# Where the low halves of delta and delta*x are subtracted in a fused Mamba and expert layer: 16 subtractions go from GpSimd to VectorE

## The chip, the cores and the metric

The kernel runs on one core of a Trainium2 chip. The time is that of the device for one execution, in microseconds. The core has TensorE (PE, matmuls into PSUM banks), VectorE (DVE), ScalarE (ACT), GpSimd (POOL), and SyncE (SP), whose queue issues most of the DMAs. The engines run side by side and meet only at semaphores; each takes its own instructions strictly in the order of the program.

## What is computed

For 32 sequences of 256 tokens with 128 channels, `x + mamba(layernorm(x)) + moe(layernorm(x))`. The heavy part is the state scan of the Mamba branch:

```python
delta = softplus(delta + dt_proj_b)
def step(s, inp):
    d_t, u_t, B_t, C_t = inp
    dA = jnp.exp(d_t[..., None] * A)
    s = s * dA + (d_t * u_t)[..., None] * B_t[:, :, None, :]
    y_t = jnp.einsum('bhdn,bhn->bhd', s, C_t)
    return (s, y_t)
```

There are 256 inner channels of 16 states each, so 4096 recurrences per sequence. The expert branch sends each token to one of 8 experts of up to 1024 tokens (two layers, 512 hidden) and weighs the result by the gate.

## The kernel before, in words

The tokens are cut in 16 chunks of 512. The main part is one body per chunk, 0 to 15, written once per kind and run in two hardware loops: body 0 alone, bodies 1 to 8 (each with one expert's matmuls besides), bodies 9 to 14 and body 15 (with the gathering of expert rows instead). I call 1 to 8 expert bodies and 9 to 15 gather bodies.

A body has 32 slots, `w` = 0 to 31, 16 for each half of the inner channels. A slot handles 128 recurrences over 512 tokens:

1. PE spreads delta*x over the 128 rows (`spread_du`, L1182) and delta (`spread_delta`, L1189), two slots ahead. Both read `dsp`, where each value stands as a high and a low part on different partitions, so that one fp32r matmul adds the two.
2. ACT takes the exponential (L762).
3. DVE multiplies delta*x by B (`spread_u`, L902, written one slot ahead) and then runs the scan (L972).
4. POOL multiplies the scanned state by C (L578). In body 0 and body 15 DVE does a share of these.
5. Every fourth slot PE sums four such products (`sum_quad`, L1204).

PE's matmuls for the next chunk's projections (L1114, L1117, L1127), for its delta (L1135 to L1138) and for the experts (L1160, L1164, L1171) stand between the slots by the hand-written tables `STAGE_A` and `FFN`. They go through two PSUM banks in turn, and a tile waits until the tile two before it was read (`claim`).

The values that `dsp` holds are made once per half chunk: ACT writes delta to `dd[:, 0]` (L720), POOL multiplies it by x into `dd[:, 1]` (L534) and clears the first step of each sequence (L538), ACT rounds both to `hi` (L726), and `lo = dd - hi` is one subtraction over 128x1024 elements. That last one is `split_low`. Then the SP queue copies both parts to `dsp` (`stack`, L434, four DMAs). The table

```python
SOFTPLUS = {"act": (2, 3, 4, 5), "scale": (9,), "zero": (10,), "low": (13,), "high": (13,)}
```

counts slots from the delta projection, so `split_low` stands at slot 7 of a body (for the second half of its own chunk, used from slot 16) and at slot 24 (for the first half of the next chunk, used from its slot 0). Who makes it was decided per body by `low_by_pool`: POOL in the expert bodies, DVE elsewhere. The very first half chunk, ahead of body 0, is POOL's.

Of the kernel before, what the change touches and what calls it, by code (L numbers as in the profile page):

```python
# [86 lines left out]
def bass_mamba_moe(nc, hidden, in_w, conv_w, conv_b, xp_w, dt_w, dt_b, a_log, d_skip, out_w,  # L87
                   wg, w1, b1, w2, b2, consts, out):
    ctx = ExitStack()
    with ctx:  # L90
# [136 lines left out]
        def softplus_slots(hf):  # L227
            v = STAGE_A[f"v{hf}"][0]
            return {what: [v + k for k in after_v] for what, after_v in SOFTPLUS.items()}

        def softplus_now(ch, w, what):

            found = []
            for hf in range(HALVES):
                at = softplus_slots(hf)[what]
                for step, slot in enumerate(at):
                    if slot % SLOTS == w:
                        of = after(ch) if slot < SLOTS else ch
                        if of[0] < CHUNKS:
                            found.append((of, hf, step))  # L240
            return found
# [21 lines left out]
        def per_chunk(ch, n, k):  # L263
            return lin(ch, lambda c: n * c + k)
# [21 lines left out]
        def wait(eng, name, value):  # L286
            if not isinstance(value, int) or value > 0:
                eng.wait_ge(S[name] if isinstance(name, str) else name, value)
# [19 lines left out]
        def delta_in(ch, hf):  # L308

            return ch if hf else before_or_start(ch)  # L310
# [4 lines left out]
        def has_ffn(ch):  # L315
            return FIRST_FFN <= ch[0] < FIRST_FFN + EXP
# [1 line left out]
        def has_combine(ch):  # L318
            return ch[0] >= FIRST_COMBINE

        def low_by_pool(ch):

            return has_ffn(ch)

        def after(ch):
            return (ch[0] + 1, ch[1])

# [3 lines left out]
        def xs_of(ch, hf):  # L331
            return xs[:, ch[0] % 2, hf, :]
# [4 lines left out]
        def head_of(w):  # L337

            return w % QUADS // 2
# [23 lines left out]
        def centre(eng, b):  # L363

            t = slice(b * BT, (b + 1) * BT)
            return eng.tensor_tensor(xn[:, t, :], acc[:, t, :], mean[:, t].unsqueeze(2).broadcast_to([P, BT, DM]),
                                     ALU.subtract)
# [137 lines left out]
        @block.gpsimd  # L505
        def _(pool):
            pool.memset(zero, 0.0).then_inc(S["zero_ready"], 1)
            pool.memset(xin, 0.0).then_inc(S["xin_zeroed"], 1)
            pool.memset(xnT[:, :, 0:TAPS - 1], 0.0).then_inc(S["xin_zeroed"], 1)
            pool.memset(weff[:, :, :], 0.0).then_inc(S["xin_zeroed"], 1)  # L510
            pool.memset(wg_sb[:, EXP:32], 0.0).then_inc(S["xin_zeroed"], 1)
            pool.memset(neg_m, -SP_M)
            pool.memset(neg_t, -SP_T)
            pool.memset(log_t1, LN_C1 - SP_M)
            pool.memset(log_t2, LN_C2 - 2 * SP_M)
            pool.memset(none, 0.0).then_inc(S["xin_zeroed"], 1)
            for b in (1, 3):
                pool.wait_ge(S["sp_chain"], 2 * b + 2)
                pool.wait_ge(S[f"x_loaded{b}"], 16)
                centre(pool, b).then_inc(S["centred_pool"], 1)  # L520
            for b in range(LN_BLK - 1):
                t = slice(b * BT, (b + 1) * BT)
                pool.wait_ge(S["rstd_ready"], b + 1)
                pool.tensor_tensor(xn[:, t, :], xn[:, t, :],
                                   rstd[:, t].unsqueeze(2).broadcast_to([P, BT, DM]),
                                   ALU.mult).then_inc(S["xn_ready"], 1)

            def scale_x(ch, hf):

                wait(pool, "stacked", per_chunk(ch, 128, 64 * hf))  # L530
                if ch == (0, None) and hf == 0:
                    pool.wait_ge(S["ein_zeroed"], 16 * EXP)
                pool.wait_ge(*tile_read(delta_in(ch, hf), f"D{hf}"))
                pool.tensor_tensor(dd[:, 1, :], dd[:, 0, :], xs_of(ch, hf), ALU.mult).then_inc(S["dx_ready"], 1)  # L534

            def zero_first():

                pool.memset(dd[:, 0, :].rearrange("p (s t) -> p s t", s=SEQS)[:, :, 0:1], 0.0  # L538
                            ).then_inc(S["dd_ready"], 1)

            def split_low(ch, hf):

                pool.wait_ge(S["hi_ready"], per_chunk(ch, 2, hf + 1))
                pool.tensor_tensor(lo, dd, hi.bitcast(F32), ALU.subtract).then_inc(S["lo_ready"], 1)

            scale_x((0, None), 0)
            pool.wait_ge(S["dx_ready"], 1)
            zero_first()
            split_low((0, None), 0)

            def gathers(tiles=range(GROUP)):

                for n in tiles:
                    pool.indirect_dma_start(back[:, n, :], None, eout[:, :],  # L554
                                            bass.IndirectOffsetOnAxis(ap=take_now[:, n:n + 1], axis=0),
                                            ).then_inc(S["back_loaded"], 16)

            def body(ch):
                for w in range(SLOTS):
                    hf, hh = w // UNITS, head_of(w)  # L560
                    if w == 1 and has_combine(ch):
                        pool.wait_ge(S["eo_free"], 16 + 32 * EXP)
                        pool.wait_ge(S["take_ready"], lin(ch, lambda c: c - FIRST_COMBINE + 1))

                    span = QUADS if ch[0] == 0 else 1
                    due = lambda what: [x for v in range(w - span + 1, w + 1) if w % span == span - 1
                                        for x in softplus_now(ch, v, what)]
                    zero_now = due("zero")
                    for of, hf_, _ in zero_now:
                        pool.wait_ge(S["dx_ready"], per_chunk(of, 2, hf_ + 1))  # L570
                    if not by_dve(ch, w):
                        if not any(by_dve(ch, v) is False for v in range(w // UNITS * UNITS, w)):
                            pool.wait_ge(*bc_loaded(ch, hf, "c"))
                        if w % UNITS == UNITS - 1 and ch[0] + 1 < CHUNKS:
                            pool.wait_ge(*tile_read(ch, f"bc{w // UNITS}"))
                        pool.wait_ge(S["scan_done"], per_chunk(ch, SLOTS, w + 1))
                        s_now = s_sb[:, w % S_RING, :]
                        pool.tensor_tensor(s_now, s_now, c_of[:, hf, hh, :], ALU.mult).then_inc(S["p_ready"], 1)  # L578
                    if zero_now:
                        zero_first()  # L580
                    if ch[0] == 0:
                        if w == 0:
                            pool.wait_ge(S["routed"], 2)
                        for i in range(w * TILES // SLOTS, (w + 1) * TILES // SLOTS):
                            pool.indirect_dma_start(ein[:, :],  # L585
                                                    bass.IndirectOffsetOnAxis(ap=put_at[:, i:i + 1], axis=0),
                                                    xn[:, i, :], None).then_inc(S["scattered"], 16)
                    for of, hf_, _ in softplus_now(ch, w, "scale"):
                        scale_x(of, hf_)
                    if low_by_pool(ch):  # L590
                        for of, hf_, _ in due("low"):
                            split_low(of, hf_)
                    if GATHER <= w < GATHER + GROUP and has_combine(ch):
                        gathers((w - GATHER,))
                    if ch[0] == CHUNKS - 1 and LAST_GATHER <= w < LAST_GATHER + GROUP:
                        if w == LAST_GATHER:
                            pool.wait_ge(S["take_ready"], TILES // GROUP)
                        gathers((w - LAST_GATHER,))

            chunks(pool, body, lambda: None)  # L600


# [187 lines left out]
        def _(dve):  # L790
# [114 lines left out]
            def split_low(ch, hf):  # L905

                dve.wait_ge(S["hi_ready"], per_chunk(ch, 2, hf + 1))
                dve.tensor_tensor(lo, dd, hi.bitcast(F32), ALU.subtract).then_inc(S["lo_ready"], 1)
# [52 lines left out]
            def body(ch):  # L961
                plan = tiles_of(ch[0])
                for w in range(SLOTS):
# [18 lines left out]
                    for step in range(2):  # L982
                        if w == GATE[step] and ch[0] > 0:
                            gate_half(before(ch), 1, step)
                        if w == UNITS + GATE[step]:
                            gate_half(ch, 0, step)
                    if not low_by_pool(ch):
                        for of, hf_, _ in softplus_now(ch, w, "low"):
                            split_low(of, hf_)
                    if has_ffn(ch) and w == b1_slot:  # L990
                        k = lin(ch, lambda c: (c - FIRST_FFN) * FT)
                        dve.tensor_copy(b1_now[:, :], b1c[:, bass.ds(k, FT)]).then_inc(S["b1_ready"], 1)
# [315 lines left out]
```

## Time and profile before

| | |
|---|---|
| median of 3 runs | 1237.58 us (1233.49 to 1238.75) |
| profiled execution | 1234.84 us, span 1232.9 us |
| busy: PE, DVE, ACT, POOL | 83%, 87%, 60%, 70% of the span |

The span runs from the first to the last instruction that the profiler saw; 1.94 us of the execution lie around it. Busy shares are means over bodies of different kinds, so they don't tell which engine is waited for in a given slot.

### The profile page before, as it was taken

The page shows a single profiled execution, that of the slowest core. Times are in us where ns is not written, and L with a number is a line of the kernel's source. Part 1 is how long each engine was busy: PE and PEld are TensorE (multiplying, and loading weights), DVE is VectorE, ACT ScalarE, POOL GpSimd, SP SyncE. Part 2 cuts the span into 40 slices and gives each one's busy share as a digit, 9 for nine tenths or more (in the row PEclk, how much of TensorE's full clock was granted, in tenths as well). Part 3 has the DMA queues.
Part 4 walks back from the last instruction along what each step waited for, and adds up shares of the span by engine and source line. Part 5 has one row for each costly group of instructions (what it writes and reads, how often), then busy time and mean ns, then how long its engine had stood idle before and what let it go on. Part 6 is the DMA issues. An engine that isn't in the chain of part 4 may idle for free.

```text
span 1232.9 us, 15308 instructions
## 1 busy us (share of the span) xinstructions
PE 1022.4 (83%) x3821; PEld 476.4 (39%) x3821; DVE 1070.5 (87%) x1331; ACT 734.7 (60%) x1117; POOL 858.9 (70%) x708
## 2 busy tenths in 40 slices
PE   0755858999999899999999997888888888888785
PEld 0522324444545454444445453333333333243322
DVE  7647968889898979899898989999898989999996
ACT  2564535767586776767685766556564756555421
POOL 2335788767676867677676769687777868686755
PEclk9988868999999999999999999788887979797765
DMA  6542325243432424342534423442434333343311
GB/s 160 157 94 68 91 79 130 57 99 69 107 80 64 103 62 111 77 94 51 119 68 98 89 57 80 86 86 48 87 71 90 81 73 68 82 85 80 72 36 34
DMA packets 81065, 103.01 MB, mean 84 GB/s; under 512 B 13280, under 2 KB 51072, under 8 KB 81024
## 3 DMA queue, kind: packets, MB, share of 16 engines
q1 hardware_dynamic: 76928, 94.18, 35.3%
q0 software_dynamic: 4096, 8.40, 2.3%
q8 instruction: 12, 0.20, 0.1%
q14 instruction: 29, 0.24, 0.1%
HBM read 18.66 MB, written 16.78 MB: 29 GB/s over the span
## 4 chain that ended last, share of the span: by engine, by line
PE 40%; DVE 24%; issue 22%; POOL 7%; ACT 3%; DVEq 1%; DMA 1%; SPq 1%; POOLq 0%; ACTq 0%
DVE u_sb L902 10%; DVE s_sb L972 8%; PE bank L1204 6%; PE bank L1171 5%; PE bank L1189 5%; PE bank L1127 4%; PE bank L1182 4%; PE bank L1114 3%; POOL expert_in L585 3%; PE bank L1135 2%; PE bank L1136 2%; PE bank L1137 2%; POOL s_sb L578 2%; PE bank L1147 2%; DVE g_sb L860 2%
## 5 line engine op out<-in xcount | busy, mean ns | idle before, releaser
L578 POOL TENSOR_TENSOR s_sb<-s_sb,c_of 128x512 f32<-128x512 f32 x480 | 628.5, 1315 | 273.2 <-DVE s_sb L972 265.1
L972 DVE TENSOR_TENSOR_SCAN s_sb<-bank,u_sb 128x512 f32<-128x512 f32 x512 | 620.4, 1212 | 0.0
L762 ACT ACTIVATE bank<-bank,a_neg 128x510 f32<-128x510 f32 x512 | 334.0, 659 | 255.9 <-PE bank L1189 246.4
L902 DVE TENSOR_TENSOR u_sb<-bank,b_of 128x512 f32<-128x512 f32 x512 | 346.2, 676 | 98.7 <-PE bank L1182 94.9
L1182 PE MATMUL bank<-dsp,sel_d 128*128 128x512 f32 x512 | 316.1, 617 | 39.8 <-DVE u_sb L902 20.4
L1189 PE MATMUL bank<-dsp,sel_d 128*128 128x512 f32 x512 | 244.5, 478 | 79.0 <-DVE s_sb L972 71.5
L1182 PEld LDWEIGHTS bank<-dsp,sel_d 128*128 128x128 f32 x512 | 104.6, 204 | 243.4 <-DVE u_sb L902 147.6
L1189 PEld LDWEIGHTS bank<-dsp,sel_d 128*128 128x128 f32 x512 | 106.5, 208 | 195.4 <-DVE s_sb L972 163.0
L1204 PE MATMUL bank<-s_sb,con 128*32 128x512 f32 x1024 | 161.2, 706 | 12.7 <-POOL s_sb L578 6.8
L1114 PE MATMUL bank<-xnT,wx 128*128 (+1 forms) x256 | 128.8, 597 | 0.0
L585 POOL DMA_INDIRECT expert_in<-xn,put_at x64 | 65.6, 1026 | 17.9 <-issue 17.8
L554 POOL DMA_INDIRECT xn<-expert_out,take_now x64 | 66.0, 1031 | 10.5 <-issue 7.4
L726 ACT ACTIVATE hi<-dd 128x1024 fp32r<-128x1024 f32 x32 | 33.9, 1058 | 61.8 <-POOL dd L538 61.8
L1127 PE MATMUL bank<-xs,bcw 128*64 128x512 f32 x64 | 46.7, 822 | 27.5 <-ACT xs L677 27.5
L1171 PE MATMUL bank<-xn 128*128 128x128 f32 x512 | 64.0, 278 | 6.4 <-ACT xn L737 6.4
L1171 PEld LDWEIGHTS bank<-xn 128*128 128x128 f32 x512 | 60.7, 191 | 17.3 <-ACT xn L737 9.9
L534 POOL TENSOR_TENSOR dd<-dd,xs 128x512 f32<-128x512 f32 x32 | 40.9, 1277 | 34.2 <-ACT dd L720 34.1
L1164 PE MATMUL bank<-xn 128*128 128x512 f32 x128 | 64.4, 605 | 0.3
L1114 PEld LDWEIGHTS bank<-xnT,wx 128*128 128x128 f32 x256 | 47.4, 189 | 27.7 <-issue 22.8
L720 ACT ACTIVATE dd<-bank,small 128x512 f32<-128x512 f32 x32 | 22.1, 690 | 52.6 <-PE bank L1138 51.6
L737 ACT ACTIVATE xn<-bank,b_now 128x512 f32<-128x512 f32 x64 | 43.1, 688 | 14.5 <-PE bank L1164 13.9
L1204 PEld LDWEIGHTS bank<-s_sb,con 128*32 128x32 f32 x1024 | 21.4, 114 | 60.0 <-issue 44.9
(140 smaller groups left out, 1045.0 us busy)
## 6 DMA issues: line engine op xcount, KB each, us to landing
b_of<-bc SPq DMA_DIRECT2D x64, 256.0 KB
c_of<-bc SPq DMA_DIRECT2D x64, 256.0 KB
dsp<-hi SPq DMA_DIRECT2D x64, 256.0 KB
dsp<-dd SPq DMA_DIRECT2D x64, 256.0 KB
expert_in<-dd SPq DMA_DIRECT2D x8, 512.0 KB, 6.4
xn<-expert_in SPq DMA_DIRECT2D x8, 512.0 KB, 5.4
xn<-L_ffn_W SPq DMA_DIRECT2D x16, 256.0 KB, 4.6
expert_out<-xn SPq DMA_DIRECT2D x16, 256.0 KB, 2.4
```

The source lines that it names most:

```text
L554: pool.indirect_dma_start(back[:, n, :], None, eout[:, :], bass.IndirectOffsetOnAxis(ap=take_now[:, n:n + 1], axis=0),).then_inc(S["back_l ...
L578: pool.tensor_tensor(s_now, s_now, c_of[:, hf, hh, :], ALU.mult).then_inc(S["p_ready"], 1)
L585: pool.indirect_dma_start(ein[:, :], bass.IndirectOffsetOnAxis(ap=put_at[:, i:i + 1], axis=0), xn[:, i, :], None).then_inc(S["scattered"], 16)
L762: act.activation(d, d, ACT.Exp, scale=a_neg[:, k:k + 1]).then_inc(S["decay_ready"], 1)
L902: dve.tensor_tensor(u_sb[:, w % U_RING, :], du_ps[w % 2][:, :], b_of[:, hf, head_of(w), :], ALU.mult).then_inc(S["u_ready"], 1)
L972: dve.tensor_tensor_scan(s_sb[:, w % S_RING, :], decay_of(w)[:, :], u_sb[:, w % U_RING, :], 0.0, ALU.mult, ALU.add).then_inc(S["scan_done" ...
L1114: mm = pe.matmul(t[:, :], wx[:, hf, part, :], xnT[:, seqs, part:part + SEQ], start=(part == 0), stop=(part == TAPS - 1))
L1127: pe.matmul(t[0:4 * NS, :] if name[0] == "b" else t[:, :], w[:, hf, :], xs_of(ch, hf), start=True, stop=True).then_inc(S["misc_pe"], 1)
L1171: mm = pe.matmul(t[:, part * P:(part + 1) * P], hT[:, f, part * P:(part + 1) * P], w2_sb[:, f, :], start=(f == 0), stop=(f == FT - 1))
L1182: pe.matmul(du_ps[w % 2][:, :], sel_d[:, group_of(w), :, :].rearrange("k n d -> k (n d)"), dsp[:, hf, head_of(w), 1, :], start=True, stop= ...
L1189: pe.matmul(decay_of(w)[:, :], sel_d[:, group_of(w), :, :].rearrange("k n d -> k (n d)"), dsp[:, w // UNITS, head_of(w), 0, :], start=True ...
L1204: mm = pe.matmul(y_ps[q * 32:(q + 1) * 32, :], con[:, K_SUM + 32 * r:K_SUM + 32 * (r + 1)], s_sb[:, (QUADS * k + q) % S_RING, :], start=(r ...
```

## The change

`low_by_pool` and its call in the GpSimd program go; the DVE program calls `split_low` in every body. The 16 subtractions of bodies 1 to 8 (two each) move. The one ahead of body 0 stays with POOL.

```diff
-        def low_by_pool(ch):
-
-            return has_ffn(ch)
...
                     for of, hf_, _ in softplus_now(ch, w, "scale"):
                         scale_x(of, hf_)
-                    if low_by_pool(ch):
-                        for of, hf_, _ in due("low"):
-                            split_low(of, hf_)
                     if GATHER <= w < GATHER + GROUP and has_combine(ch):
...
-                    if not low_by_pool(ch):
-                        for of, hf_, _ in softplus_now(ch, w, "low"):
-                            split_low(of, hf_)
+                    for of, hf_, _ in softplus_now(ch, w, "low"):
+                        split_low(of, hf_)
```

The lines move up a little in the changed file: before's L902, L908 and L972 are L895, L901 and L965 there, POOL's L578 is L574. First DVE's order at slot 7 of an expert body, before: slot 7's scan, then slot 9's product with B, then slot 8's scan.

```order
L972 SCALAR_TENSOR_TENSOR s_sb<-bank1,u_sb 128x512
L901 REGISTER_ALU
L902 TENSOR_TENSOR u_sb<-bank4,b_of 128x512
L288 REGISTER_ALU
L972 SCALAR_TENSOR_TENSOR s_sb<-bank2,u_sb 128x512
```

The same place in the changed program, where `dd<-dd,hi` is `split_low`:

```order
L965 SCALAR_TENSOR_TENSOR s_sb<-bank1,u_sb 128x512
L900 REGISTER_ALU
L901 TENSOR_TENSOR dd<-dd,hi 128x1024
L894 REGISTER_ALU
L895 TENSOR_TENSOR u_sb<-bank4,b_of 128x512
L288 REGISTER_ALU
L965 SCALAR_TENSOR_TENSOR s_sb<-bank2,u_sb 128x512
```

The subtraction now stands between slot 7's scan and slot 9's product, ahead of slot 8's scan. At slot 24 it stands in the same way, ahead of the addition that reads the expert's first output tile (`expert_out`, L880 before, L873 after):

```order
L901 TENSOR_TENSOR dd<-dd,hi 128x1024
L894 REGISTER_ALU
L895 TENSOR_TENSOR u_sb<-bank3,b_of 128x512
L965 SCALAR_TENSOR_TENSOR s_sb<-bank1,u_sb 128x512
L894 REGISTER_ALU
L895 TENSOR_TENSOR u_sb<-bank4,b_of 128x512
L965 SCALAR_TENSOR_TENSOR s_sb<-bank2,u_sb 128x512
L869 REGISTER_ALU
L871 REGISTER_ALU
L872 ISA
L873 TENSOR_TENSOR xn<-bank6,xn 128x512
```

On POOL before, it stood behind the product of slot 7 and ahead of that of slot 8; those products now follow one another.

```order
L578 TENSOR_TENSOR s_sb<-s_sb,c_of 128x512
L544 TENSOR_TENSOR dd<-dd,hi 128x1024
L576 REGISTER_ALU
L578 TENSOR_TENSOR s_sb<-s_sb,c_of 128x512
```

## Rows read from the trace of the kernel before

**Rows 1.** The page: busy us (share of the span) and instructions.

```profile
PE 1022.4 (83%) x3821; PEld 476.4 (39%) x3821; DVE 1070.5 (87%) x1331; ACT 734.7 (60%) x1117; POOL 858.9 (70%) x708
```

**Rows 2.** Groups of instructions by line, whole span: busy us, mean ns | idle before.

```profile
L544 POOL TENSOR_TENSOR dd<-dd,hi 128x1024 fp32r<-128x1024 f32 x17 | 40.1, 2358 | 1.2 <-ACT hi L726 1.2
...
L908 DVE TENSOR_TENSOR dd<-dd,hi 128x1024 fp32r<-128x1024 f32 x15 | 19.0, 1269 | 14.1 <-ACT hi L726 14.1
```

**Rows 3.** Busy by stretch: bodies 1, 2, 5 and 12 (us; PE, PEld, DVE, ACT, POOL).

```profile
184.50:258.40 73.90, 67.67 (x277) 34.73 (x276) 61.14 (x73) 47.74 (x74) 54.56 (x44) 0.94 0.38 88
258.40:328.00 69.60, 64.97 (x275) 33.15 (x274) 60.36 (x73) 47.19 (x73) 48.58 (x38) 0.98 0.38 84
...
464.10:532.20 68.10, 63.45 (x275) 32.52 (x275) 60.10 (x73) 46.97 (x73) 48.57 (x38) 1.00 0.39 85
...
943.70:1011.90 68.20, 58.46 (x187) 24.05 (x186) 63.11 (x82) 41.43 (x63) 52.76 (x44) 0.85 0.38 77
```

**Rows 4.** DVE's timeline, body 5, scans of slots 7 and 8 (start, duration).

```profile
478.03 1.21 DVE L972 TENSOR_TENSOR_SCAN s_sb<-bank,u_sb 128x512 f32<-128x512 f32 x1
...
479.74 1.21 DVE L972 TENSOR_TENSOR_SCAN s_sb<-bank,u_sb 128x512 f32<-128x512 f32 x1
```

**Rows 5.** DVE's timeline, body 12, slots 7 and 8.

```profile
958.17 1.21 DVE L972 TENSOR_TENSOR_SCAN s_sb<-bank,u_sb 128x512 f32<-128x512 f32 x1
959.30 1.24 DVE L908 TENSOR_TENSOR dd<-dd,hi 128x1024 fp32r<-128x1024 f32 x1
...
961.07 1.21 DVE L972 TENSOR_TENSOR_SCAN s_sb<-bank,u_sb 128x512 f32<-128x512 f32 x1
```

**Rows 6.** DVE's groups in 479.3 to 499.9, body 5, slots 8 to 19.

```profile
L902 DVE TENSOR_TENSOR u_sb<-bank,b_of 128x512 f32<-128x512 f32 x12 | 8.0, 668 | 0.0
```

**Rows 7.** DVE's timeline, body 5, its two longest waits, and the read at slot 26.

```profile
502.74 0.69 DVE L902 TENSOR_TENSOR u_sb<-bank,b_of 128x512 f32<-128x512 f32 x1 [2.20 <-PE bank L1182]
...
516.01 0.66 DVE L880 TENSOR_TENSOR xn<-bank,xn 128x512 f32<-128x512 f32 x1
...
521.44 0.69 DVE L902 TENSOR_TENSOR u_sb<-bank,b_of 128x512 f32<-128x512 f32 x1 [2.60 <-PE bank L1182]
```

**Rows 8.** PE's timeline, body 5.

```profile
489.82 0.49 PE L1182 MATMUL bank<-dsp,sel_d 128*128 128x512 f32 x1 [0.78 <-DMA dsp<-dd]
...
495.39 0.50 PE L1189 MATMUL bank<-dsp,sel_d 128*128 128x512 f32 x1
...
518.14 1.98 PE L1164 MATMUL bank<-xn 128*128 128x512 f32 x4
```

**Rows 9.** The SP queue's timeline, body 5, first of each `stack`.

```profile
482.93 0.51 SPq L434 DMA_DIRECT2D dsp<-hi  x1
...
517.22 0.51 SPq L434 DMA_DIRECT2D dsp<-hi  x1
```

**Rows 10.** DVE's timeline, body 1, slot 9.

```profile
206.94 0.69 DVE L902 TENSOR_TENSOR u_sb<-bank,b_of 128x512 f32<-128x512 f32 x1 [1.82 <-PE bank L1182]
```

**Rows 11.** Two stretches of body 2; third number from the end: granted clock.

```profile
271.60:275.00 3.40, 1.84 (x6) 0.56 (x5) 3.40 (x5) 3.22 (x5) 2.72 (x3) 1.00 0.00 0
275.00:278.40 3.40, 3.40 (x7) 1.60 (x8) 2.67 (x5) 2.79 (x4) 3.40 (x3) 0.50 0.07 16
```

**Rows 12.** DVE's timeline, body 2, slots 9 to 11, its waits.

```profile
277.61 0.69 DVE L902 TENSOR_TENSOR u_sb<-bank,b_of 128x512 f32<-128x512 f32 x1 [0.73 <-PE bank L1182]
...
281.89 0.69 DVE L872 TENSOR_TENSOR acc<-bank,acc 128x512 f32 x1 [0.63 <-PE bank L1147]
```

**Rows 13.** The same slots of body 12.

```profile
964.16 0.69 DVE L902 TENSOR_TENSOR u_sb<-bank,b_of 128x512 f32<-128x512 f32 x1 [0.17 <-PE bank L1182]
...
968.20 0.69 DVE L872 TENSOR_TENSOR acc<-bank,acc 128x512 f32 x1 [0.51 <-PE bank L1147]
```

**Rows 14.** POOL's timeline, body 9, the product under way as slot 7 ends.

```profile
751.30 1.29 POOL L578 TENSOR_TENSOR s_sb<-s_sb,c_of 128x512 f32<-128x512 f32 x1
```

**Rows 15.** DVE's timeline, the same moment.

```profile
752.08 1.60 DVE L908 TENSOR_TENSOR dd<-dd,hi 128x1024 fp32r<-128x1024 f32 x1
```

## The prediction

> **What bounds the kernel now.** I read the page first. VectorE is the busiest engine, 87% of the span [rows 1], and the change gives it more. A mean over the span doesn't say who waits, so I went on to the busy times by body. An expert body in the steady state takes 68.1 us, of which DVE is busy 60.10 and POOL, from which the work comes, 48.57 [rows 3]. Bodies 3 to 8 all read 68.0 to 68.2, so one of them can stand for six. Bodies 1 and 2 are longer, with a granted clock of 0.94 and 0.98 where the steady ones have 1.00.
>
> Then DVE's own timeline, to see where its 8 idle us lie. In body 5 the twelve L902 from slot 8 to slot 19 have no idle time before them [rows 6]: there DVE is the chain, one slot every 479.74 - 478.03 = 1.71 us [rows 4], and PE, ACT and POOL wait for it. The idle time comes in two lumps, 2.20 us behind slot 19 and 2.60 us behind slot 27, both ended by PE's `spread_du` [rows 7]. There PE is the chain: between the slots it works off delta and the experts' matmuls. So a body is DVE's in slots 7 to 19 and PE's from about slot 24 on, and the two subtractions fall one into each part.
>
> **What the change removes.** Sixteen L544 on POOL, 2.358 us each, 37.7 us of POOL's time [rows 2]. I cost this at nothing. L544 makes POOL's next products late by up to its own length, and DVE doesn't wait once in the slots behind it [rows 6], so PE's sums of those products never held DVE up. The work that hides it is DVE's own. If the lag did matter, the gain could be up to 2.4 us at each of the 16 places; rows 6 exclude it at slot 7.
>
> **What it adds at slot 7.** One subtraction on DVE ahead of the product and scan of slot 8. The gather bodies show this very sequence. Body 12 goes from scan 7 to scan 8 in 961.07 - 958.17 = 2.90 us [rows 5], where body 5 takes 1.71 [rows 4]. The price is 1.19 us a place. The group's mean of 1.269 [rows 2] is the busy time, which overlaps with its neighbours, and would give little more. All later work of DVE in the body is pushed back. Nobody absorbs it before slot 19, since DVE has no idle time there. Does the wait of 2.20 us behind slot 19 absorb it? I say no. PE comes to that lump from L1189 at 495.39 [rows 8], which waits for slot 16's scan: PE's burst starts when DVE lets it, so it starts 1.19 us later and ends 1.19 us later.
>
> The input `hi` should not be late. The 14.1 us of waiting for ACT before L908 [rows 2] lie in body 0, where POOL is held by the scattering of rows.
>
> **What it adds at slot 24.** The same 1.19 us, ahead of a stretch that is PE's. DVE then waits less: of the 2.60 us before L902 at 521.44 [rows 7] some is used up. Two things could let the delay through. PE's L1164 at 518.14 [rows 8] needs the bank that DVE's L880 reads at 516.01 for 0.66 us [rows 7]; 1.19 us later it ends at 517.86, 0.28 us ahead. And the SP queue stores the expert's tile before it issues `stack`; this starts at 517.22 [rows 9] and would start 1.19 us later, for matmuls that PE reaches at the end of the body. I cost slot 24 at nothing, with 1.19 us a place as the bound if that cover is gone.
>
> **What is earlier.** At slot 7 the four DMAs of `stack` begin when the low part is there, 482.93 now [rows 9] and about 480.4 then. PE waits 0.78 us for them at 489.82 [rows 8]. That wait should go, but DVE doesn't wait for PE there [rows 6], so it buys nothing.
>
> **Bodies 1 and 2.** In body 1 DVE stands idle 1.82 us at slot 9, waiting for PE [rows 10]; 1.19 us fit in, so body 1 costs 0. In body 2 the granted clock was 0.50 for 3.4 us, which is the 1.2 GHz level, after a stretch as long in which PE was busy for 1.84 us only [rows 11]. DVE then waited 0.73 + 0.63 = 1.36 us [rows 12]. The gather bodies have both the fall of the clock and DVE's subtraction at this place, and there DVE waits 0.17 + 0.51 = 0.68 us [rows 13]: a later DVE hides part of a slower PE. So body 2 costs 1.19 + 0.68 - 1.36 = 0.51.
>
> **The clock in bodies 3 to 8.** They run the same program as body 2 and show no fall; body 12 and its like do at the same slots. Which body falls depends on where it stands in time, and the change moves all of them. I take half of the six, 3 x 0.68 = 2.0 us, with bounds of none and six (4.1).
>
> **The port.** At 752.08 L908 took 1.60 us instead of 1.24 [rows 5, 15], and a product had been running on POOL since 751.30 [rows 14]: 0.36 us more. In a steady expert body POOL is up with DVE at slot 7 and its product starts after DVE's subtraction, so I add nothing; the bound is 7 x 0.36 = 2.5 us. The Trainium skill says why in *SBUF — State Buffer*, section "Who interferes with whom": a VectorE instruction with two SBUF inputs and a GpSimd instruction share one pair of ports as an exclusive lock, and the one that starts first holds it to its end. The trace agrees, and by that rule POOL's product would be the one to wait here.
>
> **The sum.** 0 (body 1) + 0.51 (body 2) + 6 x 1.19 = 7.14 (bodies 3 to 8) + 2.04 (clock) = 9.7 us. On the profiled execution's 1234.84 that is 1244.5. The median of the runs shown is 2.7 us above that execution, so 1237.58 + 9.7 = 1247.3 us, which I forecast.
>
> **The rivals.**
>
> *Hidden at slot 7 too.* If PE's burst behind slot 19 starts from something other than DVE, its 2.20 us wait absorbs the delay. Cost 0, or -0.7 if body 2's clock stays up: 1237. For it speaks that both lumps of idle time are longer than 1.19 us; against it, that L1189 at 495.39 waited for DVE. Chance 0.12.
>
> *Faster: the low part was late.* PE waits 0.78 us for `dsp` at slot 16. If this is the chain in each of the eight bodies, 8 x 0.78 = 6.2 us come back and DVE's delay is hidden: 1231.3. It decides if DVE is found waiting for PE's spread of slot 16. In body 5 it isn't. The Trainium skill speaks for this side in *GPSIMD Engine Reference*, section "4.1 Engine selection": two-input elementwise work belongs on VectorE, GpSimd being about half as fast. The rows agree on the ratio, 2358 to 1269 ns [rows 2], but what is gained in engine time is on the engine with room. Chance 0.05.
>
> *Exposed at slot 24 too.* If 0.28 us is too little, or the late `stack` is waited for, 8 x 1.19 = 9.5 us come on top: 1256.8. Chance 0.07.
>
> *The clock falls nearly everywhere.* DVE's late slots leave PE idle in more pieces. If the six steady bodies lose 1.36 us each as body 2 did, without overlap, that is 8.2 in place of 2.0: 1253.4. Body 12's 0.85 [rows 3] shows that the level isn't safe; that PE has 5 us more work in an expert body speaks against. Chance 0.13.
>
> **How the numbers follow.** The forecast's own case has 0.60 and spans +7.7 (no fall of the clock) to +11.7 (six), 1245.3 to 1249.3; 0.03 is left for what I don't see. Three runs of before spread over 5.3 us, so I widen: 1241 leaves out the two low rivals (0.17) and 1254 the one at 1256.8. Half a per cent, 6.2 us, is about what a measurement can tell from no change. Slower takes the rivals above and nearly all of the main case, 0.60 x 0.9 + 0.20 = 0.74; within 0.5% the rest of it and the hidden case, 0.21; faster 0.05.
>
> **What would show it.** In the changed trace: sixteen more of the 128x1024 subtraction on DVE at 1.20 to 1.27 us, only one on POOL; scan 7 to scan 8 of a steady body 2.9 us apart; still no idle time of DVE from slot 8 to 19 except where the clock fell; the 2.20 us wait unchanged and the 2.60 us wait shorter by about 1.2; the 0.78 us wait for the DMA gone; bodies 3 to 8 at 69.2 to 70.0 us; gather bodies as before. The forecast is wrong if the wait behind slot 19 shrinks instead, if the one behind slot 27 doesn't, or if the clock's falls cost more than 4 us.

## The result and the profile after

| | before | after |
|---|---|---|
| median of 9 runs | 1234.63 us (1231.19 to 1238.75) | 1243.37 us (1240.41 to 1245.73) |
| profiled execution | 1234.84 us, span 1232.9 us | 1241.68 us, span 1239.7 us |

The ratio is 1.0066 with an interval of 1.005 to 1.0082: the changed kernel is slower, by 8 to 9 us (the medians differ by 8.7). The forecast was 1247.3 us within 1241 to 1254. Of the 3.9 us by which it lies above the measured median, 3.0 are the median of before itself, which six more runs brought down from 1237.58 to 1234.63; the forecast's +9.7 on the new median would be 1244.3. The two profiled executions differ by 6.8 us.

The page of after answers to [rows 1]: DVE has 16 instructions and 14.8 us more, POOL 16 instructions and 21.7 us less, and the span is longer all the same. The sixteen instructions that left POOL took 37.7 us, yet its busy time fell by 21.7 only: its products (L578 before, L574 after) have become 15.0 us longer in sum. The two lines below are theirs.

```profile
PE 1021.3 (82%) x3821; PEld 479.1 (39%) x3821; DVE 1085.3 (88%) x1347; ACT 734.9 (59%) x1117; POOL 837.2 (68%) x692
```

```profile
L578 POOL TENSOR_TENSOR s_sb<-s_sb,c_of 128x512 f32<-128x512 f32 x480 | 628.5, 1315 | 273.2 <-DVE s_sb L972 265.1 <-POOL dd L534 3.5 <-DMA expert_out<-xn 1.0
...
L574 POOL TENSOR_TENSOR s_sb<-s_sb,c_of 128x512 f32<-128x512 f32 x480 | 643.5, 1344 | 301.5 <-DVE s_sb L965 295.5
```

The groups of the subtraction, answering to [rows 2]: 31 on DVE at a mean of 1253 ns, one left on POOL.

```profile
L901 DVE TENSOR_TENSOR dd<-dd,hi 128x1024 fp32r<-128x1024 f32 x31 | 38.9, 1253 | 14.1 <-ACT hi L719 14.1
...
L540 POOL TENSOR_TENSOR dd<-dd,hi 128x1024 fp32r<-128x1024 f32 x1 | 2.3, 2347 | 1.2 <-ACT hi L719 1.2
```

Then the busy times of after by body, answering to [rows 3]: bodies 1, 2, 3, 4, 5, 7 and 12 (columns as there). The steady expert bodies (4 and 5 here) have gone from 68.0 and 68.1 to 69.0 and 69.1 (69.2 in the rounded window) at a granted clock of 1.00. Bodies 3 and 7 took 69.7 at 0.98. Body 12 takes 68.2 as before.

```profile
184.90:257.40 72.50, 66.51 (x277) 33.80 (x276) 63.52 (x75) 47.70 (x74) 51.83 (x42) 0.96 0.38 89
257.40:326.40 69.00, 64.02 (x275) 32.50 (x274) 62.17 (x75) 47.00 (x73) 45.92 (x36) 1.00 0.39 84
326.40:396.10 69.70, 65.08 (x275) 33.78 (x275) 62.36 (x75) 47.01 (x73) 45.90 (x36) 0.98 0.38 83
396.10:465.10 69.00, 64.01 (x275) 32.50 (x274) 62.18 (x75) 47.01 (x73) 45.91 (x36) 1.00 0.39 84
465.10:534.30 69.20, 64.25 (x275) 32.60 (x275) 62.27 (x76) 47.11 (x73) 45.87 (x36) 1.00 0.38 83
...
603.30:673.00 69.70, 65.09 (x275) 33.69 (x275) 62.35 (x75) 47.11 (x73) 45.93 (x36) 0.98 0.38 83
...
949.70:1017.90 68.20, 57.70 (x188) 24.36 (x187) 63.01 (x82) 41.42 (x63) 52.67 (x44) 0.88 0.37 77
```

DVE's timeline of after in body 5, answering to [rows 4, 7]. The first three lines are slot 7; then the wait behind slot 19, the read of the expert's bank at slot 26, and the wait behind slot 27.

```profile
479.05 1.22 DVE L965 TENSOR_TENSOR_SCAN s_sb<-bank,u_sb 128x512 f32<-128x512 f32 x1
480.18 1.20 DVE L901 TENSOR_TENSOR dd<-dd,hi 128x1024 fp32r<-128x1024 f32 x1
...
481.89 1.22 DVE L965 TENSOR_TENSOR_SCAN s_sb<-bank,u_sb 128x512 f32<-128x512 f32 x1
...
504.80 0.69 DVE L895 TENSOR_TENSOR u_sb<-bank,b_of 128x512 f32<-128x512 f32 x1 [2.18 <-PE bank L1174]
...
519.20 0.68 DVE L873 TENSOR_TENSOR xn<-bank,xn 128x512 f32<-128x512 f32 x1
...
523.48 0.69 DVE L895 TENSOR_TENSOR u_sb<-bank,b_of 128x512 f32<-128x512 f32 x1 [1.88 <-PE bank L1174]
```

Scan 7 to scan 8 is 481.89 - 479.05 = 2.84 us, 1.13 more than before. The wait behind slot 19 is 2.18 where it was 2.20: PE came later by the same amount, and nothing was absorbed there. The wait behind slot 27 fell from 2.60 to 1.88. That is not all that slot 24 was paid with, since a wait of 0.34 us behind slot 26 went as well, 1.06 together. Between the lumps DVE still never stands, as in [rows 6]; the twelve products of slots 8 to 19, from the groups of that stretch:

```profile
L895 DVE TENSOR_TENSOR u_sb<-bank,b_of 128x512 f32<-128x512 f32 x12 | 8.1, 679 | 0.0
```

PE's timeline of after in the same body, answering to [rows 8]. PE's spread of slot 16 has no wait for the DMA any more; the expert's next tile starts at 520.19.

```profile
491.19 0.49 PE L1174 MATMUL bank<-dsp,sel_d 128*128 128x512 f32 x1
...
520.19 1.98 PE L1156 MATMUL bank<-xn 128*128 128x512 f32 x4
```

The SP queue of after, answering to [rows 9]: the first `stack` begins 481.41 - 465.1 = 16.3 us into the body, where it began 482.93 - 464.1 = 18.8 us into it.

```profile
481.41 0.51 SPq L430 DMA_DIRECT2D dsp<-hi  x1
...
520.41 0.51 SPq L430 DMA_DIRECT2D dsp<-hi  x1
```

Two stretches of body 3 of after, to be read like [rows 11]. The same pattern that body 2 of before had now stands here: PE busy for 1.84 us only, then the 1.2 GHz level for 3.3 us.

```profile
340.60:344.00 3.40, 1.84 (x5) 0.44 (x4) 3.40 (x4) 3.37 (x4) 2.52 (x2) 1.00 0.07 16
344.10:347.40 3.30, 3.30 (x13) 2.75 (x12) 3.30 (x5) 1.88 (x4) 2.48 (x2) 0.50 0.99 221
```

Stretch by stretch the profiled executions differ so (lengths from the starts of the scans of slot 0):

| | forecast | after minus before |
|---|---|---|
| up to body 1 | 0 | +0.3 |
| body 1 | 0 | -1.4 (73.9 to 72.5) |
| body 2 | +0.5 | -0.5 (69.59 to 69.04) |
| bodies 3 to 8, slot 7 | +7.1 | +6.1 (1.02 each) |
| bodies 3 to 8, clock | +2.0 | +1.1 (bodies 3 and 7, 0.55 each) |
| bodies 9 to 15 | 0 | +1.2 (body 9 +0.6, body 15 +0.9) |
| sum | +9.7 | +6.8 |

### The profile page after: what moved, and what is told of

Same layout as the page of the kernel before. It is cut to its first block, busy times and chain, and to the rows that moved or that the text cites. A ratio compares the mean times of both kernels' runs of the same rounds, so it can differ in the third digit from the quotient of the medians.

```text
span 1239.7 us, 15316 instructions
## 1 busy us (share of the span) xinstructions
PE 1021.3 (82%) x3821; PEld 479.1 (39%) x3821; DVE 1085.3 (88%) x1347; ACT 734.9 (59%) x1117; POOL 837.2 (68%) x692
## 4 chain that ended last, share of the span: by engine, by line
PE 38%; DVE 26%; issue 23%; POOL 5%; ACT 4%; DMA 2%; DVEq 1%; SPq 1%; POOLq 0%; ACTq 0%
DVE u_sb L895 11%; DVE s_sb L965 7%; PE bank L1196 5%; PE bank L1163 5%; PE bank L1181 4%; PE bank L1174 4%; PE bank L1106 3%; PE bank L1119 3%; PE bank L1127 3%; PE bank L1139 2%; POOL expert_in L581 2%; PE bank L1128 2%; PE bank L1129 2%; DVE g_sb L853 2%; POOL s_sb L574 1%
## 5 line engine op out<-in xcount | busy, mean ns | idle before, releaser
L574 POOL TENSOR_TENSOR s_sb<-s_sb,c_of 128x512 f32<-128x512 f32 x480 | 643.5, 1344 | 301.5 <-DVE s_sb L965 295.5
L965 DVE TENSOR_TENSOR_SCAN s_sb<-bank,u_sb 128x512 f32<-128x512 f32 x512 | 622.1, 1215 | 0.0
L895 DVE TENSOR_TENSOR u_sb<-bank,b_of 128x512 f32<-128x512 f32 x512 | 347.7, 679 | 89.2 <-PE bank L1174 88.5
L1174 PE MATMUL bank<-dsp,sel_d 128*128 128x512 f32 x512 | 312.2, 610 | 37.2 <-DVE u_sb L895 21.9
L1181 PE MATMUL bank<-dsp,sel_d 128*128 128x512 f32 x512 | 242.5, 474 | 89.5 <-DVE s_sb L965 83.5
L1174 PEld LDWEIGHTS bank<-dsp,sel_d 128*128 128x128 f32 x512 | 103.2, 202 | 235.6 <-DVE u_sb L895 155.5
L1181 PEld LDWEIGHTS bank<-dsp,sel_d 128*128 128x128 f32 x512 | 104.7, 204 | 210.3 <-DVE s_sb L965 182.6
L1196 PE MATMUL bank<-s_sb,con 128*32 128x512 f32 x1024 | 156.6, 687 | 12.7 <-POOL s_sb L574 8.5
L1119 PE MATMUL bank<-xs,bcw 128*64 128x512 f32 x64 | 44.0, 777 | 27.4 <-ACT xs L670 27.4
L901 DVE TENSOR_TENSOR dd<-dd,hi 128x1024 fp32r<-128x1024 f32 x31 | 38.9, 1253 | 14.1 <-ACT hi L719 14.1
```

The source lines that it names most:

```text
L895: dve.tensor_tensor(u_sb[:, w % U_RING, :], du_ps[w % 2][:, :], b_of[:, hf, head_of(w), :], ALU.mult).then_inc(S["u_ready"], 1)
L965: dve.tensor_tensor_scan(s_sb[:, w % S_RING, :], decay_of(w)[:, :], u_sb[:, w % U_RING, :], 0.0, ALU.mult, ALU.add).then_inc(S["scan_done" ...
L1119: pe.matmul(t[0:4 * NS, :] if name[0] == "b" else t[:, :], w[:, hf, :], xs_of(ch, hf), start=True, stop=True).then_inc(S["misc_pe"], 1)
L1174: pe.matmul(du_ps[w % 2][:, :], sel_d[:, group_of(w), :, :].rearrange("k n d -> k (n d)"), dsp[:, hf, head_of(w), 1, :], start=True, stop= ...
L1181: pe.matmul(decay_of(w)[:, :], sel_d[:, group_of(w), :, :].rearrange("k n d -> k (n d)"), dsp[:, w // UNITS, head_of(w), 0, :], start=True ...
L1196: mm = pe.matmul(y_ps[q * 32:(q + 1) * 32, :], con[:, K_SUM + 32 * r:K_SUM + 32 * (r + 1)], s_sb[:, (QUADS * k + q) % S_RING, :], start=(r ...
```

## The experiments

My theory: the whole effect is the subtraction at slot 7, which lengthens a chain of DVE's own work, and slot 24's is hidden by DVE's wait for PE. The rivals: the two places share the effect; or the cost lies in when the low part is ready. All kernels but e8 and e9 share one edit of before, a rule that names the slots as well. The runs of before on the same chips had medians of 1235.37 us (e1 to e4), 1235.47 (e5 to e8) and 1236.21 (e9, e10).

```diff
-        def low_by_pool(ch):
-            return has_ffn(ch)
+        def low_by_pool(ch, w):
+            return ...
```

### One place at a time: e1 and e2

e1, slot 7 of the expert bodies on DVE, slot 24 left to POOL:

```diff
+            return has_ffn(ch) and w != 7
```

> Only the eight subtractions of slot 7 in bodies 1 to 8 go to DVE; those of slot 24 stay with POOL. My theory: slot 7 is the whole cost, so this takes as long as the changed kernel: +6 to +9 us over before, scan 7 to scan 8 of a steady body 2.85 us apart, a steady body 69.0 to 69.7 us. Rival, that both places share the cost or slot 24 bears it: +4 us or less.

e2, the other way round:

```diff
+            return has_ffn(ch) and w == 7
```

> Only the eight subtractions of slot 24 in bodies 1 to 8 go to DVE; those of slot 7 stay with POOL. My theory: hidden behind PE's work, 0 +- 1.5 us, the waits behind slots 26 and 27 fall from 0.34 + 2.60 to about 1.9 us and a steady body stays at 68.0 to 68.1 us. Rival, that DVE pays wherever it works: +8 x 1.13 = +9 us.

| | median us | ratio | bodies 2 to 8 |
|---|---|---|---|
| e1 | 1242.25 | 1.006 [1.0044, 1.0076] | 69.0, 69.7, 69.0, 69.1, 69.0, 69.7, 69.0 |
| e2 | 1236.2 | 1.0013 [1.0, 1.0027] | 68.0, 68.1, 68.0, 68.1, 68.0, 68.1, 68.0 |

e1 alone has the changed kernel's loss within the intervals, and e2, whose interval just reaches 1.0, next to nothing; its bodies are as long as before's. The windows row of e2 for body 8 shows where its subtraction went: DVE is busy for 60.99 us in 68.00. DVE's waits in such a body sum to 6.8 us, where before's bodies have 7.9; those behind slots 26 and 27 went from 0.34 + 2.60 to 1.90, as expected.

```profile
669.00:737.00 68.00, 63.17 (x275) 32.48 (x274) 60.99 (x75) 46.97 (x72) 46.88 (x37) 1.00 0.39 84
```

### Does the cover of slot 24 have an end: e3

e2, with a spare subtraction of 768 elements ahead of the real one, into a tile that nobody reads:

```diff
...
+                            if has_ffn(ch) and w == 24:
+                                w_ = wx[:, :, :, :].rearrange("p h k m -> p (h k m)")
+                                dve.tensor_tensor(spare[:, :], w_[:, 0:768], w_[:, 256:1024], ALU.subtract)
                             split_low(of, hf_)
```

> As the run with slot 24 alone on DVE, with one more DVE subtraction of 768 elements per partition (about 0.85 us, two SBUF inputs, its result goes unused) ahead of each of these eight. Theory A, the cover at slot 24 is limited by the bank that PE's first hidden-layer matmul waits for: it had 0.28 us to spare before 1.14 us came on top in full, so DVE's read of the expert tile now ends about 0.6 us after PE is ready, and each of the 8 bodies grows by 0.5 to 0.8 us, +4 to +6 us in all. Theory B, the cover is the whole wait of DVE (0.34 + 2.60 = 2.94 us, of which 2.0 are used): 0 +- 1.5 us.

Measured: 1254.17 us, 1.0145 [1.0123, 1.0167], +18 us. The sign and the place were right, the size was missed by three times. DVE's timeline of e3, body 5, slot 24:

```profile
519.91 1.22 DVE L973 TENSOR_TENSOR_SCAN s_sb<-bank,u_sb 128x512 f32<-128x512 f32 x1
521.04 0.94 DVE L992 TENSOR_TENSOR spare<-wx 128x768 f32<-128x768 f32 x1
521.89 2.30 DVE L909 TENSOR_TENSOR dd<-dd,hi 128x1024 fp32r<-128x1024 f32 x1
...
524.72 1.21 DVE L973 TENSOR_TENSOR_SCAN s_sb<-bank,u_sb 128x512 f32<-128x512 f32 x1
```

and POOL's at the same moment:

```profile
521.21 1.90 POOL L579 TENSOR_TENSOR s_sb<-s_sb,c_of 128x512 f32<-128x512 f32 x1 [0.43 <-DVE s_sb L973]
```

The real subtraction took 2.30 us instead of 1.2: the times fit POOL's product having been issued during the spare one, having waited for it, and having run ahead of the second. So DVE was delayed by 524.72 - 519.91 - 1.71 = 3.10 us, not by the two that I had counted. PE's timeline shows what stopped it:

```profile
525.98 0.50 PE L1193 MATMUL bank<-dsp,sel_d 128*128 128x512 f32 x1 [0.55 <-DVE s_sb L973]
...
528.28 1.98 PE L1168 MATMUL bank<-xn 128*128 128x512 f32 x4 [0.80 <-DVE xn L881]
```

This tile waits for the bank that DVE's `expert_out` reads, the very hazard that the prediction priced at 0.28 us of room with one subtraction. In before DVE's read ended at 516.01 + 0.66 = 516.67 and the tile began at 518.14 [rows 7, 8], 1.47 us of room for 3.10 us of delay, which leaves 1.6. PE had lost 0.55 us of that already to a wait for DVE's scan at 525.98; the tile's wait ends last and covers it. Body 4 of e3, in which the clock stayed up, took 69.7 us: 1.6 more than before's 68.0. The other steady ones took 71.2 to 71.4 at a mean clock of 0.98, so there the clock adds about 1.6 a body. The cover ends where the prediction put it. Behind its end the clock doubled the price in six of seven bodies; why it falls in these isn't shown.

### Is POOL's lateness or the time of the low part worth anything: e6 and e5

e6 leaves out the subtraction at slot 7 of bodies 1 to 8 but for 2 of every 512 columns, which DVE makes, so that neither engine carries it:

```diff
+                            if has_ffn(ch) and w == 7:
+                                dve.wait_ge(S["hi_ready"], per_chunk(of, 2, hf_ + 1))
+                                dve.tensor_tensor(lo[:, :, 0:2], dd[:, :, 0:2], hi.bitcast(F32)[:, :, 0:2],
+                                                  ALU.subtract).then_inc(S["lo_ready"], 1)
```

> The kernel before with slot 7's subtraction of bodies 1 to 8 left out but for 2 of 512 columns, made on DVE (so the low part is the whole value there and the output isn't the reference's). POOL is rid of 2.36 us and the low part is there 2.3 us earlier, at a cost to DVE of about 0.1 us. My theory, that neither POOL's lateness nor the time of the low part is on the chain: 0 to +2 us against before, steady bodies 68.0 to 68.3 us. Rival, that the low part was late on POOL: 8 x 0.78 = -6 us.

Measured: 1234.6 us, 0.9995 [0.998, 1.0009]. Bodies 2 to 8 took 68.0 or 68.1 but for body 3 with its fall of the clock (69.7). Taking 2.36 us from POOL and having the low part early (`stack` starts 15.2 us into body 5 and not 18.8) buys nothing. The windows row of e6 for body 5: POOL is down to 46.39 us, and the body is as long as in [rows 3].

```profile
463.80:531.90 68.10, 63.51 (x275) 32.48 (x274) 60.12 (x75) 46.98 (x73) 46.39 (x37) 1.00 0.39 85
```

e5 takes the changed kernel and puts the second half's subtraction four slots later:

```diff
+                        if has_ffn(ch):
+                            due_low = softplus_now(ch, 7, "low") if w == 11 else [x for x in due_low if w != 7]
```

> The changed kernel with the second half's subtraction of bodies 1 to 8 at slot 11 of DVE instead of slot 7, so that the low part and its DMAs are about 7 us later than in the changed kernel and 4.4 us later than in the one before. It measures how much room the low part had. From the traces: the subtraction ends at about 23.1 us into a body, its four DMAs take 6.9 us, so PE's spread of slot 16 starts at about 30.1 and DVE's product of slot 16, due at about 28.8, at 30.5. My theory, that the low part had room of some microseconds: each body grows by 1 to 2 us over the changed kernel's, +8 to +16 us over the changed kernel (+17 to +25 over before). Rival, that the low part is already the chain at slot 7: +7 us per body, some +56 us.

Measured: 1274.56 us, 1.0323 [1.0298, 1.0348], +39 us, between the two theories. PE's timeline of e5, body 5, the spread of slot 16, the first that reads the new values:

```profile
512.38 0.79 PE L1185 MATMUL bank<-dsp,sel_d 128*128 128x512 f32 x1 [4.06 <-DMA dsp<-dd]
```

and DVE's waits that follow it, where before has none:

```profile
513.20 0.69 DVE L902 TENSOR_TENSOR u_sb<-bank,b_of 128x512 f32<-128x512 f32 x1 [2.01 <-PE bank L1185]
...
516.22 0.69 DVE L902 TENSOR_TENSOR u_sb<-bank,b_of 128x512 f32<-128x512 f32 x1 [1.20 <-PE bank L1185]
...
518.48 0.69 DVE L902 TENSOR_TENSOR u_sb<-bank,b_of 128x512 f32<-128x512 f32 x1 [0.38 <-PE bank L1185]
```

A late low part does reach DVE. PE waits 4.06 us for the DMA; 3.6 of them arrive at DVE, its wait behind slot 19 grew from 2.18 to 3.02 too, and the clock fell to a mean of 0.95 in half of the bodies and 0.98 in the others. In this body `stack` starts 23.1 us in, where it is 18.8 in before and 16.3 in after. Before's room can be read: PE's spread of slot 16 ended at 489.82 + 0.49 = 490.31 [rows 8], and DVE's product of that slot begins 1.5 us later, in DVE's timeline of before:

```profile
491.83 0.66 DVE L902 TENSOR_TENSOR u_sb<-bank,b_of 128x512 f32<-128x512 f32 x1
```

The 0.78 us that PE waits in before had been spent ahead of that. My size for e5 missed because PE's order puts slot 16's spread ahead of work that slot 15 needs, and because the clock followed.

### The opposite change in the gather bodies: e4

If a subtraction on DVE at slot 7 costs 1 us a body, giving slot 7 of bodies 9 to 15 to POOL should bring it back. In bodies 1 to 8 e4 is like e2.

```diff
+            return ch[0] > 0 and w == 7
```

> Slot 7's subtraction is made by POOL in all bodies 1 to 15, slot 24's by DVE in all. In bodies 9 to 15 this takes 1.19 us per body from DVE's chain but puts 2.36 us on POOL, which issues gathers there and is up to 3.8 us late already. Theory A, POOL's lateness stays hidden: -7 x 1.19 = -8 us against before. Theory B, PE's sum of units 8 to 11 waits for POOL and takes the gain back: -2 us to +8 us, with a wait of PE L1204 for POOL L578 of 1 us or more in each gather body.

Measured: 1252.55 us, 1.0134 [1.0117, 1.0151], +16.6 us: both theories missed. Bodies 10 to 14 took 71.2 to 72.1 us instead of 68.2. POOL's timeline of e4, body 12:

```profile
971.80 2.36 POOL L544 TENSOR_TENSOR dd<-dd,hi 128x1024 fp32r<-128x1024 f32 x1
974.32 0.99 POOL L554 DMA_INDIRECT xn<-expert_out,take_now  x1 [0.16 <-issue]
975.32 1.30 POOL L578 TENSOR_TENSOR s_sb<-s_sb,c_of 128x512 f32<-128x512 f32 x1
...
977.78 7.42 POOL L578 TENSOR_TENSOR s_sb<-s_sb,c_of 128x512 f32<-128x512 f32 x6
```

and DVE's combining (`combine`, two inputs in SBUF) at slots 14 and 15:

```profile
981.95 3.42 DVE L893 SCALAR_TENSOR_TENSOR acc<-xn,gate,acc 128x128 f32 x1
...
987.01 0.32 DVE L893 SCALAR_TENSOR_TENSOR acc<-xn,gate,acc 128x128 f32 x1
```

POOL, which also issues eight gathers in this half, fell behind and made up for it with six products back to back. The first combining instruction of DVE fell into that run and took 3.42 us instead of 0.32, up to the end of POOL's run at 985.20 (981.95 + 3.42 = 985.37). DVE lost 3.1 us at the port, the pair of SBUF ports that it shares with POOL, where it had saved 1.2. So in this kernel a subtraction on POOL is free only where POOL has caught up before DVE next reads two SBUF operands.

### Room for the opposite change: e7 to e10

e8 moves the gathers of bodies 9 to 14 from slots 1 to 8 to slots 9 to 16, and the combining from 14 to 21 to 19 to 26, with nothing of the change in it; e7 does so and gives slot 7 to POOL.

```diff
+LATE_GATHER, LATE_COMBINE = 9, 19
...
-                        if COMBINE <= w < COMBINE + GROUP:
-                            ins = combine(ch, w - COMBINE)
+                        if combine_at(ch) <= w < combine_at(ch) + GROUP:
+                            ins = combine(ch, w - combine_at(ch))
```

> The kernel before with only the gathers of bodies 9 to 14 moved to slots 9 to 16 and their use to slots 19 to 26; no subtraction moves. It is the control of the run with both. Theory A: DVE does the same work and PE the same, so 0 +- 2 us. Theory B: combining behind slot 19, where DVE waits for PE, is hidden in part: -2 to -6 us.

> POOL makes slot 7's subtraction in bodies 1 to 14, DVE slot 24's; in bodies 9 to 14 the gathers stand in slots 9 to 16 instead of 1 to 8 and their use by DVE in slots 19 to 26 instead of 14 to 21, so that POOL is not late at slot 7. Theory A, DVE's chain in slots 7 to 19 is shorter by 1.14 us in each of six gather bodies and POOL's products of slots 9 to 16 don't hold it: -5 to -8 us against before. Theory B, the gathers make POOL late in slots 9 to 18, and DVE's combining instructions, which have two SBUF inputs, meet POOL's products and wait for the shared port: 0 or slower.

Measured: e8 1270.67 us, 1.0288 [1.0261, 1.0316]; e7 1269.7, 1.0288 [1.0261, 1.0315]. e8 missed; e7's rival had the sign, but not the main cause, which both share. It is shown by POOL's last gather and DVE's first combining instruction of e8, body 12, slot 19: the last gathers, issued between products by a late POOL, hadn't landed.

```profile
1000.17 0.99 POOL L561 DMA_INDIRECT xn<-expert_out,take_now  x1 [0.16 <-issue]
...
1006.17 0.35 DVE L900 SCALAR_TENSOR_TENSOR acc<-xn,gate,acc 128x128 f32 x1 [6.41 <-DMA xn<-expert_out,take_now]
```

That wait (6.2 to 6.9 us a body) hides what slot 7 is worth, so e7 and e8 tell nothing about the change. e9 moves only the combining, to slots behind the wait at slot 19 (23 and 25 to 31), with the gathers at their old place:

```diff
+LATE_COMBINE = (23, 25, 26, 27, 28, 29, 30, 31)
...
-                        if COMBINE <= w < COMBINE + GROUP:
-                            ins = combine(ch, w - COMBINE)
+                        if w in combine_slots(ch):
+                            ins = combine(ch, combine_slots(ch).index(w))
```

> The kernel before with only DVE's combining of gathered rows in bodies 9 to 14 moved from slots 14 to 21 to slots 23 and 25 to 31; the gathers stay in slots 1 to 8, no subtraction moves. Theory, that DVE pays in slots 7 to 19 and not behind: six of the eight instructions (0.26 us each) leave the part where DVE is the chain, and 2.6 us of waiting for PE behind slots 27 and 31 take most of the eight: -1.5 us a body, -6 to -12 us in all. Rival, that DVE's work costs the same in every slot: 0 +- 1.5 us.

e10 has that combining, the gathers at slots 9 to 16, and slot 7 of bodies 1 to 14 on POOL:

> As the run with the late combining, and in bodies 9 to 14 the gathers in slots 9 to 16, and slot 7's subtraction on POOL in bodies 1 to 14 (slot 24's on DVE everywhere). The 6.4 us for which DVE waited for the last gather when it combined from slot 19 should be gone, since the last gather is issued 40 us into a body and slot 23 comes at about 47. Theory A: another -1.14 us a body against the run with the late combining alone, -12 to -18 us against before. Theory B, POOL's lateness of 4 to 5 us in slots 14 to 19 meets DVE's gate multiplication of two SBUF inputs at the shared port or PE's sums: nothing gained, 0 or slower than the late combining alone.

Measured: e9 1232.31 us, 0.9972 [0.9952, 0.9991]; e10 1239.48, 1.0023 [1.001, 1.0037]. e9 is the fastest kernel of the study, 3.9 us (0.3%) under before. Its gain was two thirds of the least that I expected, and not the one that I expected: body 9 fell from 70.7 to 67.3 and body 10 from 68.2 to 67.9, while 11 to 14 stayed at 68.2 or 68.3. Most of the 3.4 us of body 9 is the port's. In before the first combining instruction of that body fell into a run of POOL's products, as in e4, and took 3.07 us where that of body 12 took 0.33:

```profile
761.92 7.44 POOL L578 TENSOR_TENSOR s_sb<-s_sb,c_of 128x512 f32<-128x512 f32 x6
...
766.44 3.07 DVE L893 SCALAR_TENSOR_TENSOR acc<-xn,gate,acc 128x128 f32 x1
```

In e9 all eight take 0.32. DVE's timeline of e9 in body 9 shows one long wait, behind slot 19:

```profile
735.61 0.69 DVE L910 TENSOR_TENSOR u_sb<-bank,b_of 128x512 f32<-128x512 f32 x1 [0.22 <-PE bank L1190]
739.45 0.69 DVE L910 TENSOR_TENSOR u_sb<-bank,b_of 128x512 f32<-128x512 f32 x1 [0.30 <-PE bank L1190]
772.69 0.69 DVE L910 TENSOR_TENSOR u_sb<-bank,b_of 128x512 f32<-128x512 f32 x1 [1.87 <-PE bank L1190]
```

In bodies 11 to 14 the theory of e9 failed. PE comes to the burst behind slot 19 from the release by slot 16's scan, so of the instructions that left slots 14 to 21 only those of slots 14 and 15 can bring it forward: in body 12 slot 20's scan came 0.5 us earlier against slot 14's than in before, as slot 16's did, and the wait behind slot 19 grew from 0.84 to 1.86 for the rest. The wait of 1.26 us behind slot 27 was used up, and four of the moved instructions, at slots 28 to 31, gave the gain back.

In e10 POOL's products start up to 5.0 us behind the end of their scan in body 12 and 6.7 in body 10 (slots 13 to 19), and bodies 9 to 14 take 68.7 to 69.6 us. Its rival held: in body 13 PE waits 2.07 us for a product of POOL, and DVE's wait behind slot 19 is 5.67 us (1.87 in e9); in body 12 DVE's gate multiplication, of two SBUF inputs, took 1.47 us instead of 0.67. Nothing is gained, but since e8 has POOL as late without the subtraction (4.9 us in body 12), the moved gathers do this, and what the subtraction is worth there is open.

## Why the prediction was right

**What the change removes is worth nothing: right.** The 37.7 us of instructions that POOL lost buy no time. e6, where neither engine has the subtraction at slot 7, takes as long as before.

**Slot 7: the mechanism right, the price slightly high.** I gave it 1.19 us a place, from the gather bodies. The gap between the scans grew by 1.13, 0.09 of it came back between the scans of slots 11 and 12, and the bodies are 1.0 longer (68.0 to 69.0). The wait behind slot 19 kept its 2.2 us, the check that told this case from the rival *hidden at slot 7 too*. e1 alone gives +6.9 us, the whole effect within the intervals.

**The picture of DVE's idle time: incomplete, without harm.** The prediction saw two lumps, 4.80 of DVE's 7.9 us of waiting. There is a third, 1.49 us behind slot 31, which PE's expert matmul L1171 ends; in after it is 1.49 too. And DVE's chain ends with slot 16's scan and not with slot 19, as e9 shows in the gather bodies; slot 7 lies ahead of both.

**Slot 24 at nothing: right, with the room as stated.** In after DVE's read ends at 519.20 + 0.68 = 519.88, and PE's tile starts at 520.19: 0.31 us of room, where the prediction had 0.28. e2 shows the place hidden, e3 that it stops being hidden when the delay passes that room. The wait behind slot 27 shrank by 0.72 and not by 1.2, since the wait behind slot 26 gave 0.34.

**The low part was late: excluded.** The `stack` starts 2.5 us earlier in the body and the 0.78 us wait is gone, as forecast, and neither helped. e5 shows that this path exists, with 1.5 us of room left in before and, since `stack` starts earlier, more in after.

**The clock: counted as a risk, sized at 2.0, found at 1.1.** Two of the six bodies fell, not three, and each cost 0.55 us, near the 0.68 from the gather bodies. The reason given, that a later DVE hides part of a slower PE, is borne out: where DVE has no subtraction at slot 7 a fall costs 1.6 us (body 3 of e6, body 2 of before). That the mean over executions can be had from one of them is not shown. Up to body 8, e8 and e9 are the same program as before. e8 had 74.0 and 69.6 us in bodies 1 and 2, much like before (73.9 and 69.6), and e9 had 72.0 and 68.0. So the -1.4 and -0.5 of the table are falls that before's profiled execution happened to have and after's had shorter or not at all. They are no gain of the change. They sum to -1.9, as much as lies between 6.8, the difference of the profiled executions, and 8.7, that of the medians; that this is the reason is not shown. On the nine-run median the total came within 1 us partly by luck: the slot 7 term and the clock were each about 1 us too high, and body 2, body 9 and body 15 went their own ways.

**Body 2 at +0.5: wrong, the step was the clock's.** I priced it on the fall of the clock being there after the change too; it wasn't. Without a fall in either kernel the body goes from 68.0 (e9) to 69.0 (after), the same 1.0 as the others. Body 1 at 0 holds by the same comparison: 72.0 in e9 and 72.0 in e1.

**The gather bodies at nothing: off by 1.2 us in the profiled execution.** Their program is unchanged. Body 9 took 70.7 us in before and anything from 70.6 to 72.1 in e1 to e3 and e6; body 15 84.5 in before and 85.4 in after, e1, e2, e3 and e6, but 84.5 in e9. In body 9 part of it is the port: the first combining instruction took 3.07 us in before and 2.14 in after. What decides the rest is open.

**The port: right in direction, no cost.** At slot 7 DVE's subtraction started 0.16 us ahead of POOL's product, and it was the product that became longer, as the timeline of POOL in after shows (1.27 us is usual). All sixteen products at these places took 2.2 us, which is nearly all of the 15.0 us of the result:

```profile
480.34 2.17 POOL L574 TENSOR_TENSOR s_sb<-s_sb,c_of 128x512 f32<-128x512 f32 x1 [0.68 <-DVE s_sb L965]
```

This is what the Trainium skill says in *SBUF — State Buffer*, "Who interferes with whom": whoever starts first holds the shared pair of ports until its instruction ends. Nobody waits for that product within the 0.9 us. The opening said that the engines meet only at semaphores; these two meet at the port as well.

The Trainium skill's advice in *GPSIMD Engine Reference*, "4.1 Engine selection", to put two-input elementwise work on VectorE, speaks for this change. The trace bears out its ratio (2358 to 1253 ns) and the runs show its limit here: the sum of DVE's and POOL's busy time fell by 6.9 us, the kernel got slower.

## What to carry to other kernels

Before moving an instruction to a faster engine, look at whether that engine has any idle time between the place and the next point at which it waits for another: with none, nearly the whole duration goes on the end (1.02 of 1.20 us here), and the wait further on may stay as long as it was if the engine waited for is itself started by this one. Where there is such a wait, it hides the instruction only up to the earliest consumer, so work out the room in tenths of a us. And taking load off the slower engine was worth nothing by itself here; its load counted where its backlog met a shared port.

## What the runs showed of the hardware

- **The shared port, in numbers.** A DVE instruction with two SBUF inputs that came while a product was under way on POOL took 1.79 us (after, body 1, in the timelines below) and 2.30 us (e3) instead of 1.20, and through a back-to-back run of products 3.42 us instead of 0.32 (e4). In e4, and in body 9 of before, DVE's instruction came out only behind the last of the queued products; in body 1 of after it came out behind the one under way, and the next product took 2.25 us. What decides between the two is open. The other way round POOL's product took 2.17 us instead of 1.27. Of two such DVE instructions in a row the second came out behind a product of POOL (e3), 1.1 us later than alone.
- **The clock's falls differ between executions of the same instructions.** Bodies 1 and 2 lost 2.0 and 1.6 us to them in e8 against e9 (mean granted clock 0.94 and 0.98 in e8, 0.96 and 1.00 in e9). A fall cost a body 0.55 us where DVE makes slot 7's subtraction (after), and 1.6 where it doesn't (before, e3, e6).
- **Gathers issued between products.** POOL issued one every 2.45 us, 0.99 of it the issue itself. DVE had waited for 0.4 us when the last of eight was issued at 1000.17, and went on 6.0 us later (e8, body 12).

```profile
199.71 5.13 POOL L574 TENSOR_TENSOR s_sb<-s_sb,c_of 128x512 f32<-128x512 f32 x3
...
201.92 1.79 DVE L901 TENSOR_TENSOR dd<-dd,hi 128x1024 fp32r<-128x1024 f32 x1
```
